# The term D times x moved from a diagonal product on TensorE to a product on GpSimd and a per-head add on VectorE

## The reference

```python
zxbcdt = x @ W_in
z, xBC, dt = split(zxbcdt)
xBC = silu(conv(xBC)); xh, Bmat, Cmat = split(xBC); dt = softplus(dt + dt_bias)
Y_diag = einsum('bcln,bcsn,bhcls,bcshp->bclhp', Cc, Bc, Lmat, xdt)
Y_off  = einsum('bcln,bchpn,bhcl->bclhp', Cc, prevs, exp(A_cum))
Y = Y_diag + Y_off + xh * D[:, None]
Y = Y * silu(z);  Y = Y * rsqrt(mean(Y * Y) + EPS) * norm_w
out = (Y @ W_out) @ W_lin + b_lin
```

## Time and profile before

| | us |
|---|---|
| median of 3 runs (788.69 to 790.18) | 789.65 |
| the profiled execution's own time | 790.98 |
| its span | 789.2 |
| TensorE busy (matmul) | 744.3, 94% |
| VectorE busy | 725.7, 92% |
| ScalarE busy | 672.1, 85% |
| GpSimd busy | 632.1, 80% |

### The profile page before, as it was taken

One profiled execution on the slowest core, in us unless ns is written; L12 is line 12 of the kernel. 1 busy time (PEld: TensorE's weight loads), 2 busy tenths in 40 slices (PEclk: granted clock), 3 DMA queues, 4 the chain that ended last, 5 costly groups with the idle time before them and its releaser, 6 DMA issues.

```text
span 789.2 us, 21076 instructions
## 1 busy us (share of the span) xinstructions
PE 744.3 (94%) x6049; PEld 711.4 (90%) x6049; DVE 725.7 (92%) x1898; ACT 672.1 (85%) x1428; POOL 632.1 (80%) x1215
## 2 busy tenths in 40 slices
PE   3679999999999999878899999999999999999987
PEld 1379999999999999877899999999999999999976
DVE  6999999999999998697999999999989899999986
ACT  5999898989899898964888888888888898989864
POOL 5582788888888888886888888888888888888863
PEclk9979999999999999999999999999999999999999
DMA  7689888989898986032211212121212121210000
GB/s 217 187 244 333 276 281 284 313 268 347 250 329 278 315 283 251 1 72 68 67 64 45 69 45 68 43 66 43 66 43 68 45 69 40 70 41 18 10 4 15
DMA packets 97961, 110.43 MB, mean 140 GB/s; under 512 B 6865, under 2 KB 89713, under 8 KB 97905
## 3 DMA queue, kind: packets, MB, share of 16 engines
q1 hardware_dynamic: 97906, 109.78, 43.4%
HBM read 90.87 MB, written 18.89 MB: 139 GB/s over the span
## 4 chain that ended last, share of the span: by engine, by line
PE 75%; DVE 9%; POOL 7%; ACT 4%; issue 3%; DMA 1%; POOLq 0%; DVEq 0%; ACTq 0%
PE accA L1701 26%; PE accC L1710 25%; PE ps L1640 3%; PE ps L1808 3%; PE ps L1792 3%; PE ps L1825 2%; PE ps L1806 2%; PE ps L1790 2%; PE ps L1810 2%; PE ps L1844 2%; DVE code L777 2%; PE ps L1817 1%; DVE maskC L785 1%; PE ps L1827 1%; DMA adj_in<-in_adj_dram 1%
## 5 line engine op out<-in xcount | busy, mean ns | idle before, releaser
L1338 ACT ACTIVATE maskA<-code 128x1024 fp32r<-128x1024 int8 x256 | 269.2, 1053 | 22.0 <-DVE code L777 17.0
L1701 PE MATMUL accA<-Y,maskA 128*128 128x260 f32 (+1 forms) x1792 | 270.5, 294 | 1.3 <-issue 1.1
L1710 PE MATMUL accC<-Y,maskC 128*128 128x260 f32 (+1 forms) x1792 | 253.0, 284 | 6.0 <-DVE maskC L785 6.0
L1701 PEld LDWEIGHTS accA<-Y,maskA 128*128 128x128 f32 x1792 | 232.9, 191 | 4.5 <-issue 2.1
L1710 PEld LDWEIGHTS accC<-Y,maskC 128*128 128x128 f32 x1792 | 228.7, 189 | 7.1 <-DVE maskC L785 7.0
L785 DVE TENSOR_SCALAR maskC<-code 128x1024 fp32r<-128x1024 int8 x256 | 205.5, 803 | 0.1
L777 DVE SCALAR_TENSOR_TENSOR code<-f_rows,neg_f,ps 128x512 int8<-128x512 int8 (+1 forms) x256 | 178.2, 739 | 1.8 <-PE ps L1640 0.5
L1275 ACT ACTIVATE edges<-adj_in 128x1024 int8<-128x1024 f32 x128 | 135.3, 1059 | 2.4 <-DMA adj_in<-in_adj_dram 2.3
L638 POOL TENSOR_TENSOR room_r<-room,room_r 128x256 fp32r<-128x256 f32 x128 | 97.7, 791 | 2.5
L1063 DVE SCALAR_TENSOR_TENSOR room<-room 128x128 f32<-128x128 f32 x270 | 86.2, 340 | 0.0
L1640 PE MATMUL ps<-ident,edges 128*128 128x128 bf16 x512 | 51.3, 225 | 11.0 <-ACT edges L1275 11.0
(11 more groups left out here) (275 smaller groups left out, 1627.6 us busy)
## 6 DMA issues: line engine op xcount, KB each, us to landing
adj_in<-in_adj_dram SPq DMA_DIRECT2D x128, 512.0 KB, 5.1
edge_codes<-code SPq DMA_DIRECT2D x32, 512.0 KB, 5.6
code<-edge_codes SPq DMA_DIRECT2D x32, 512.0 KB, 3.3
xn<-in_x_dram SPq DMA_DIRECT2D x4, 512.0 KB, 5.7
room<-in_x_dram SPq DMA_DIRECT2D x32, 64.0 KB, 1.8
room<-in_L_gnn_h_dram SPq DMA_DIRECT2D x32, 64.0 KB, 2.0
out_dram<-room SPq DMA_DIRECT2D x32, 64.0 KB, 1.6
room<-in_L_ffn_W_in_dram SPq DMA_DIRECT2D x1, 192.0 KB, 2.5
```

Source lines behind the costliest of these rows:

```text
L1338: s.activation(maskA[:, b % MASKS], src, ACT.Relu, bias=1.0 - LINK, scale=-1.0).then_inc(S["maskA_ready"], 1)
L1701: t_.matmul(accA[k][:, 0:2 * cols], maskA[:, b % MASKS, l * P:(l + 1) * P], y2_of(jt, 0) if cols == F else Y[:, jt, 0, :, 0:cols], start=j ...
L1710: m = t_.matmul(accC[k][:, 0:2 * cols], maskC[:, b % MASKS, l * P:(l + 1) * P], y2_of(jt, 1) if cols == F else Y[:, jt, 1, :, 0:cols], sta ...
```

## The change

ScalarE copies the turned x of a chunk from ps[2] to a buffer `skip` (128 x 256, two of them) at the end of `x_times_dt`. GpSimd multiplies the buffer in place with D, broadcast over the 64 columns of each head (`skip_product`, after `decayed_state`). VectorE replaces the one L1030 by four operations, one for each head, which multiply the state's part by the decay and add the buffer. The two L1806 go; each head's product starts its own accumulation. `d_row` (D on all partitions, one DMA) takes the place of `d_col` (two DMAs) and of `skip_w`. The order of `drain` on GpSimd gets four products.

```diff
-        d_col = rows_space.take(KB)
+        d_row = rows_space.take(NH)
...
-        skip_w = adj_space.take(KB, P)
+        skip = adj_space.take(2, DI)
...
-            for dst, src, n in ((b_row, b_lin, P), (dt_b, dt_bias, NH), (a_row, A_log, NH)):
+            for dst, src, n in ((b_row, b_lin, P), (dt_b, dt_bias, NH), (a_row, A_log, NH), (d_row, D, NH)):
                 sp.dma_start(dst, src.rearrange("(o c) -> o c", o=1).broadcast_to([P, n])).then_inc(S["w_in"], 16)
-            heads_of = D.rearrange("(k h) -> h k", h=P // HD)
-            for h in range(P // HD):
-                sp.dma_start(d_col[h * HD:(h + 1) * HD], heads_of[h:h + 1].broadcast_to([HD, KB]),
-                             allow_slow_non_contiguous=True).then_inc(S["w_in"], 16)
...
+            def skip_product(c, kc):
+
+                wait(pool, "skip_in", c + 1)
+                g.tensor_tensor(heads(skip[:, kc], HD), heads(skip[:, kc], HD), d_row.unsqueeze(2).broadcast_to([P, NH, HD]),
+                                ALU.mult).then_inc(S["skip_ready"], 1)
...
                 if ok[2]:
                     decayed_state(s_ - 3, (k - 3) % 2)
+                    skip_product(s_ - 3, (k - 3) % 2)
...
             def drain():
                 a, b, c, d = range(LAST - 3, NT)
+                skip_product(a, a % 2)
                 second_rstd(d)
                 decayed_state(a, a % 2)
                 split_dam(c, c % 2)
                 x1_with_bias(c, c % SLOTS)
                 decayed_state(b, b % 2)
+                skip_product(b, b % 2)
                 norm_scale(a)
                 split_dam(d, d % 2)
                 decayed_state(c, c % 2)
+                skip_product(c, c % 2)
                 x1_with_bias(d, d % SLOTS)
+                skip_product(d, d % 2)
...
-                dve.wait_ge(S["w_in"], 16 * 13)
+                dve.wait_ge(S["w_in"], 16 * 12)
...
-                for kb in range(KB):
-                    v.tensor_scalar(skip_w[:, kb], ident[:], d_col[:, kb:kb + 1], None, ALU.mult).then_inc(S["skip_ready"], 1)
...
                 wait(dve, "yg_ready", c)
-                scaled_off = step(v.tensor_tensor(heads(ysum), heads(ps[0][:, DI:2 * DI]),
-                                                  tiny[:, 4 + kc, 0:NH].unsqueeze(2).broadcast_to([P, NH, HD]), ALU.mult))
+                dve.wait_ge(S["skip_ready"], c + 1)
+                for h in range(NH):
+                    mine = slice(h * HD, (h + 1) * HD)
+                    scaled_off = step(v.scalar_tensor_tensor(out=ysum[:, mine], in0=ps[0][:, DI + h * HD:DI + (h + 1) * HD], scalar=tiny[:, 4 + kc, h:h + 1],
+                                                             in1=skip[:, kc, mine], op0=ALU.mult, op1=ALU.add))
...
                     m.then_inc(S["xl_ready"], 1)
+                wait(act, "y_read", c - 1)
+                s.copy(skip[:, kc], ps[2][:, P:P + DI]).then_inc(S["skip_in"], 1)
...
-                if isinstance(c, int) and c == 0:
-                    pe.wait_ge(S["skip_ready"], KB)
                 for kb in range(KB):
-                    t_.matmul(ps[0][:, kb * P:(kb + 1) * P], xbc[:, kc, kb, :], skip_w[:, kb], start=True, stop=False)
                     for h in range(kb * P // HD, (kb + 1) * P // HD):
-                        t_.matmul(ps[0][:, h * HD:(h + 1) * HD], mix_of(c)[:, h], xdt[:, h * HD:(h + 1) * HD], start=False,
-                                  stop=h == (kb + 1) * P // HD - 1)
+                        t_.matmul(ps[0][:, h * HD:(h + 1) * HD], mix_of(c)[:, h], xdt[:, h * HD:(h + 1) * HD], start=True,
+                                  stop=True)
```

More of the change, by code:

```diff
@@ L236, in gnn_ffn_kernel @@
             zt_ready nv_ready ew_ready dt_ready dam_ready conv_pre ctan_ready conv_ready halo_done gate_done
-            mix_ready xdt_ready  ps_ready y_read yg_ready st_done skip_ready yT_ready ssq_ready rs_ready
+            mix_ready xdt_ready  ps_ready y_read yg_ready st_done skip_in skip_ready yT_ready ssq_ready rs_ready
             exp_done out_done zcopy cT_ready bl_ready last_feat w_joined""".split()
@@ L695, in drain @@
                 end_chain()
-            pool.wait_ge(S["w_in"], 16 * 13)
+            pool.wait_ge(S["w_in"], 16 * 12)
             schedule(g, slot)
@@ L1589, in slot @@
                 if isinstance(s_, int) and s_ == 0:
-                    act.wait_ge(S["w_in"], 16 * 13)
+                    act.wait_ge(S["w_in"], 16 * 12)
                     s.activation(a_row, a_row, ACT.Exp).then_inc(S["w_ready"], 1)
@@ L1761, in turn_weights @@
             def turn_weights():
-                pe.wait_ge(S["w_in"], 16 * 13)
+                pe.wait_ge(S["w_in"], 16 * 12)
                 for kb in range(KB):
```

## The result

| | us |
|---|---|
| median before (788.69 to 790.18, 4 runs) | 789.18 |
| median after (800.73 to 804.81, 4 runs) | 801.78 |
| ratio | 1.0164, 95% interval 1.0147 to 1.0182 |
| the profiled execution, before and after | 790.98 and 800.73 |
| its span, before and after | 789.2 and 799.0 |

The change costs 12.6 us; the forecast was +5.4. The direction held and the size did not.

The account below looks back on a forecast made before the run. TensorE bounds the second pass at 12.97 a slot; VectorE's chain would grow to 13.15. Pass +4.9, opening -0.4, drain +0.9 make +5.4 us: 795.1 as a median, own range 791.5 to 799, with far ends 785 to 803.

Parts of the forecast that it names:

- the bound: Second pass: TensorE is busy in all of its 12.97 us a slot, so it bounds this stretch.
- the place of the new wait: TensorE idles before L1833, the turning of the gated y, until VectorE's gating ends; about 0.6 a slot.
- the chain through VectorE: Input products, copy, taps, gating, turning: 12.50 us a slot before, 12.94 with the heads, 13.15 with GpSimd's product.
- the heads: VectorE: four per-head operations of 64 columns, 0.20 each and 0.78 together, replace L1030's 0.34; +0.44 a slot.
- I take what one such meeting costs L1089, 0.21: Head of the taps: GpSimd's new product holds up VectorE by 0.21 a slot, bounds 0 and 0.61.
- "much slower" rival: Head of the taps: GpSimd's product costs VectorE its whole 0.61, chain 13.55, total 805.8; chance 0.15.
- the hand-over of 0.03 between gating and turning: Loop over the engines: a hand-over costs 0.03, read from ScalarE to VectorE, in 8.62 + 0.03 + 3.85 = 12.50.
- covered, barely: ScalarE: the new copy's 0.25 fits in 0.28 of room left before TensorE needs the next xn2.
- GpSimd has long waits there, which hide its four products: Drain: GpSimd's products cost nothing; only the heads count, 0.44 x 2 = +0.9.
- The faster rival: Second pass: VectorE's chain stays below TensorE's 12.53, so TensorE bounds; 778.3, a part of it near 784; chance 0.15.

Follow-up runs that it names:

- e12: Kernel before without the diagonal products, plus GpSimd's product on a zero buffer nobody reads, old single scaling, term left out: 798.20 us, ratio 1.0118.
- e11: Kernel before without the diagonal products, plus ScalarE's copy alone; no GpSimd product, old single scaling, term left out: 792.21 us, ratio 1.0044.
- e13: Kernel before without the diagonal products, with four per-head operations adding zeros; no copy, no product, term left out: 793.68 us, ratio 1.0076.
- e4: Kernel before, diagonal products kept, with four per-head operations adding zeros in place of the one scaling; no copy, no product: 795.08 us, ratio 1.0083.
- e2: Changed kernel with the old single scaling in place of the four per-head operations; copy and product stay, term not added: 802.80 us, ratio 1.0180.
- e1: Changed kernel without GpSimd's product; VectorE adds ScalarE's copy as it stands, so D is left out: 792.76 us, ratio 1.0047.
- e3: Kernel before with only the diagonal products taken away; no copy, no product, one scaling, term left out: 786.70 us, ratio 0.9972.
- e10: Complete version of the change without GpSimd's product: TensorE turns x with D's diagonal, ScalarE scales by dt / D; 795.35 us, ratio 1.0078 against the kernel before.
- e6: Changed kernel with the drain's last GpSimd product placed behind the output's scale (norm_scale of chunk b): 802.34 us.

## Why the prediction was wrong in size

**Right: the bound, the place of the new wait, the heads.** TensorE bounded the pass, the chain through VectorE became longer than TensorE's own work, and TensorE now waits at the turning of the gated y, ended by the gating. Heads: +0.44 forecast, +0.43 measured, 0.19 to 0.20 each. The closeness is partly luck: 0.27 - 0.065 is 0.205, so the prediction's own slope gives 0.82 and +0.48 for four, not the 0.78 and +0.44 that it went on with. The Trainium skill's figure for PSUM sources ("VectorE: DVE Perf Modes", TRN2 errata) gave +0.375; the measured +0.43 lies between it and that +0.48. The ScalarE copy took 0.25, as forecast.

**Wrong: "I take what one such meeting costs L1089, 0.21".** This is the term that failed most. L1089 is such a meeting, as the prediction read it; in the kernel before GpSimd's L609 runs beside it:
```profile
606.59 0.58 POOL L609 TENSOR_TENSOR featw<-xn,row_out 128x128 f32 x1
606.82 0.39 DVE L1089 TENSOR_TENSOR room<-room 128x20 f32<-128x20 f32 x1
```
L1089 ends 0.03 to 0.04 after L609 in each of 24 slots there. It is issued with 0.35 of L609 left, and that is all that its 0.39 tells. The distance is the same in every kernel of this study (L609 starts 0.23 to 0.24 earlier), so L1089 keeps its length, and its 0.21 is the price of this one place, not of a meeting anywhere. What a meeting costs is the time that is left of GpSimd's operation: at the head of the taps that came to +0.41 in the changed kernel and +0.66 in e12. The prediction also looked at the product alone and not at what it pushes: L658 ended 0.02 after L1053 began in the kernel before, and any delay put it over the first tap. The Trainium skill says this on a page that the prediction did not use ("SBUF — State Buffer", "SBUF: two separate sides"): VectorE and GpSimd share a pair of ports by an exclusive lock, an operation of VectorE with two SBUF inputs takes part in it, and whoever comes second is blocked until the other's operation is over. e12 agrees, to 0.02 us; the per-head operations, with one input from PSUM, were not stretched beside a busy GpSimd, which agrees as well. The "much slower" rival had this mechanism, with the whole 0.61 as its price, and was given 0.15.

**Wrong: the hand-over of 0.03 between gating and turning.** That row was from ScalarE to VectorE. From VectorE to TensorE it is 0.11 to 0.12, in e11, e13, e4 and the changed kernel alike. So the chain is 9.46 + 0.11 + 3.80 = 13.37 for 13.15: +0.20 from the meeting, +0.08 from the hand-over, -0.05 on TensorE's part and -0.01 from the heads.

**Wrong: "covered, barely" for the ScalarE copy.** The prediction looked for the copy's cost at the next xn2 and found 0.28 of room. The copy lies on a loop that wasn't in it, from the taps' end over ScalarE to the output product: 12.67 before the change, 0.30 under TensorE's pace, 12.90 with the copy. In the changed kernel it is 7.19 + 3.53 + 0.11 + 2.45 = 13.28, within 0.1 of the loop over the gating. So taking the heads away buys nothing (e2), and only what relieves both loops does: the product (e1).

**Wrong: "GpSimd has long waits there, which hide its four products".** The drain cost +3.0, not +0.9. The heads were sized right: e4's end stretch is +1.0. The products were not free. GpSimd is on the chain of the kernel before from the last slot's taps to the next mix (chain that ended last):
```profile
747.85 0.29 POOL room L626
...
753.57 2.52 POOL room_r L638 x4
```
Up to VectorE's L1160 (L1167 after), the silu that releases the last cumulation, e4 (heads alone) is 0.48 behind the kernel before, e12 (product alone) 1.05, e11 (copy alone) 0.39 and the changed kernel 1.37. From there come +0.82 in the clock's low stretch, +0.73 up to the output of b and +0.11 to the end, 3.03 together. The 0.82 is not the product's: e1 has no product, and its low stretch lies over the same way, which takes 3.0 there, so that its end stretch is 47.3.

**The sum again.** Forecast: +4.9 pass, -0.4 opening, +0.9 drain. Measured: +9.25, -2.5 (of which the removed L959 explain 0.4 at most; the rest varies between runs), +3.0. The missing 4.35 of the pass is 0.17 a slot; an ordinary slot is 0.2 over the forecast, by the meeting and the hand-over, and every fourth takes 13.7 in most of the pass (13.08 before) with one of 13.1 behind it, while some at its ends take 13.2.

**The faster rival** (778.3) had no chance: e3, with every cost of the change removed, is 786.70. TensorE's 0.44 a slot was never there to be had, since GpSimd's dense work moves into the taps and the loop over ScalarE is next. The prediction gave this case 0.15 for the prices of the heads; what decided was elsewhere.

**What stays open:** why every fourth slot, where the program's loop begins anew, lengthens more than the others (13.7 after, 13.3 in e11; from the output product to the next slot's start TensorE takes 2.8 to 2.9 there for 2.45, behind both loops); what delays the taps in e10's longest slots; the 4 us between after's own runs; and the opening's 3.5 us between profiles. The late output of b in e6 was not traced further than to ScalarE's L1560.

## What to carry to other kernels

When one engine bounds by half a microsecond a slot, write out every loop that closes over the slot (here gating to turning, and tanh to output product) with its own hand-overs before pricing an edit; a change gains only what the second longest leaves. Put no work on GpSimd just ahead of a stretch of VectorE operations with two SBUF inputs: ask also what the new operation pushes, as here L659. A price of contention read at one place is what was left of the other engine's operation there; at a new place it has to be worked out anew, from where both operations start.

## What the runs showed of the hardware that was not expected

- An operation of VectorE with two SBUF tensors that is issued into one of GpSimd with two SBUF tensors stands still until that is over: four columns took 0.17 alone, 0.27, 0.37 and 0.58 in the changed kernel, e3 and e12, each time to within 0.03 us after the end of GpSimd's operation. A tap of 128 columns ends 0.14 to 0.16 after it. L1089 shows the same in every slot, in the kernel before too. That GpSimd stands still the same way when it comes second is not shown by these lines.
- From the end of a VectorE operation to the start of TensorE's weight load that waits for it: 0.11 to 0.12 us; from ScalarE's copy to TensorE 0.11; from ScalarE to VectorE 0.03.
- TensorE's granted clock was 1.00 through the pass and about 0.5 to 0.6 for some 4 us in the drain of most kernels (0.55 and 0.60 before, 0.58 and 0.57 after, by two-us pieces), after a stretch in which TensorE was busy 5.50 of 8 us (before) or 4.54 of 8 (after). In e3 (5.06 of 8) and e12 (4.65 of 8) it stayed at 1.00, and their drains, 44.6 and 45.6, are among the shortest. Where it lies moved the way from cumulation to mix by 0.8 us (2.87 against 2.05). The changed kernel has a second, earlier dip in its drain (0.94 in the 17 us from 750.7 and in the 10 us from there on), which the kernel before has not; e13 has one too and comes to the last silu only 0.04 behind e4, which has none.
